# Fused four-layer graph network on one core: the tile pairs of the last layer in two interleaved streams, each with its own accumulation bank

## The reference

```
deg = jnp.maximum(adj.sum(axis=1, keepdims=True), 1e-08)
w = adj / deg
log_ij = _logmap(x[:, None, :], x[None, :, :], c)
agg = jnp.einsum('ij,ijc->ic', w, log_ij)
transformed = agg @ weight + bias
origin = jnp.zeros_like(transformed)
return _expmap(origin, transformed, c)
```

## Time and profile before

| | us |
|---|---|
| median of 3 runs (1842.58 to 1855.55) | 1851.97 |
| the profiled execution | 1837.7 |
| its span in the profile | 1835.9 |
| PE busy / DVE busy / ACT busy / POOL busy | 1602.7 / 1369.7 / 908.6 / 296.4 |
| first sum (L1849) of the last layer's loop, start | 1303.23 |
| last sum, start | 1774.94 |
| first of the final transposes (L1021), start | 1787.83 |

### The profile page before, as it was taken

The page is one execution under the profiler, slowest core; times in us unless marked ns, Lnnn a source line. Parts: engine busy times, 40 slices in busy tenths (PEclk is TensorE's granted clock), DMA queues, the critical chain, the costliest instruction groups (busy, mean ns, idle before and its releaser), DMA issues.

```text
span 1835.9 us, 21795 instructions
## 1 busy us (share of the span) xinstructions
PE 1602.7 (87%) x8154; PEld 660.7 (36%) x8198; DVE 1369.7 (75%) x1602; ACT 908.6 (49%) x870; POOL 296.4 (16%) x190
## 2 busy tenths in 40 slices
PE   6999999999997899999999863876789999999990
PEld 2433333333334344434334332332432333333340
DVE  4777799978885666785885945997447778878877
ACT  2233567733333323333332314221547789988964
POOL 1000000000000122111120200000423334444440
PEclk9999999999997899999999996998556779989995
DMA  9999599849994255243343110336012435454610
GB/s 351 412 413 413 206 374 392 335 151 414 413 393 186 95 181 183 93 140 135 137 146 119 55 46 13 137 126 206 12 47 80 138 127 195 149 182 139 202 40 23
DMA packets 118012, 348.72 MB, mean 190 GB/s; under 512 B 6244, under 2 KB 31144, under 8 KB 117672
## 3 DMA queue, kind: packets, MB, share of 16 engines
q1 hardware_dynamic: 106784, 329.27, 48.7%
q10 hardware_dynamic: 11144, 18.34, 2.7%
HBM read 329.76 MB, written 17.83 MB: 189 GB/s over the span
## 4 chain that ended last, share of the span: by engine, by line
PE 44%; DVE 26%; issue 16%; POOL 9%; ACT 2%; DMA 1%; SPq 0%; DVEq 0%; POOLq 0%; ACTq 0%
PE ps L751 10%; POOL ring L648 9%; PE ps L821 9%; PE ps L828 6%; DVE work L1476 5%; DVE work L1725 4%; DVE work L1513 4%; PE ps L684 3%; PE ps L683 3%; PE ps L924 2%; PE ps L796 2%; DMA ring<-in_adjT 1%; DVE ring L1681 1%; DVE work L1678 1%; PE ps L800 1%
## 5 line engine op out<-in xcount | busy, mean ns | idle before, releaser
L821 PE MATMUL ps<-ring,stage_f 128*64 128x512 f32 x512 | 264.2, 598 | 33.8 <-DVE ring L1681 29.3
L823 PE MATMUL ps<-work,stage_f 128*64 128x512 f32 x512 | 264.2, 598 | 0.0
L1084 ACT ACTIVATE work<-ps,code_bias 128x1024 uint8<-128x1024 f32 x128 | 135.7, 1110 | 243.6 <-PE ps L684 237.0
L1170 ACT ACTIVATE work<-ring 128x2048 f32<-128x2048 f32 x64 | 122.3, 1913 | 236.9 <-PE ps L830 230.5
L648 POOL TENSOR_TENSOR ring<-ring,work 128x1024 f32<-128x1024 f32 x80 | 189.4, 2367 | 286.2 <-DVE work L1842 232.9
L828 PE MATMUL ps<-work,stage_words 128*64 128x512 bf16 x768 | 208.3, 380 | 0.0
L830 PE MATMUL ps<-work,stage_words 128*64 128x512 bf16 x768 | 208.3, 380 | 0.0
L924 PE MATMUL ps<-work 69*128 69x512 f32 x320 | 192.6, 732 | 1.9 <-DVE work L1768 1.9
L621 POOL COPY stage_f<-X 128x256 f32 (+1 forms) x32 | 30.9, 964 | 952.4 <-ACT work L1046 583.8
L751 PE MATMUL ps<-ring,work 128*64 128x512 f32 x704 | 160.8, 598 | 0.0
L828 PEld LDWEIGHTS ps<-work,stage_words 128*64 128x64 bf16 x768 | 84.8, 110 | 178.1 <-issue 153.4
(11 more groups left out here) (289 smaller groups left out, 2910.5 us busy)
## 6 DMA issues: line engine op xcount, KB each, us to landing
ring<-in_adjT SPq DMA_DIRECT2D x90, 2048.0 KB, 10.8
work<-in_adjT SPq DMA_DIRECT2D x26, 2048.0 KB, 13.0
ring<-in_adjT SPq DMA_DIRECT2D x48, 1024.0 KB, 7.1
codes<-work ACTq DMA_DIRECT2D x64, 256.0 KB, 6.2
work<-codes SPq DMA_DIRECT2D x32, 512.0 KB, 3.6
ring<-in_adjT SPq DMA_DIRECT2D x32, 512.0 KB, 3.8
X<-in_x ACTq DMA_DIRECT2D x1, 1024.0 KB, 5.0
work<-in_xT SPq DMA_DIRECT2D x2, 512.0 KB, 22.4
```

Of the source, the lines that this page charges most:

```text
L821: nc.tensor.matmul(ps[0:F, h, :], stage_f[:, t, k, 0:F], ring[:, r, k, cols], start=start, stop=stop)
L823: nc.tensor.matmul(ps[F:P, h, :], stage_f[:, t, k, 0:F], negs[:, pair, i, cols], start=start, stop=stop)
L1084: nc.scalar.activation(codes[:, u, k:k + 2, :].rearrange("p k c -> p (k c)"), ps[:, bank:bank + 2, :].rearrange("p k c -> p (k c)"), ACT.Relu,
L1170: nc.scalar.activation(negs[:, pair], ring[:, s % RING, 2 * pair:2 * pair + 2, :], ACT.Relu, scale=-1.0).then_inc(negs_made, 1)
```

## The change

The units are now two streams, 48 off (O) and 32 own (D), each sorted by I, and taken in the pattern O O D O D from the first to the last five, which are O O O D D. So units of different I are mixed. Each stream accumulates its gathers in a bank of its own: off in bank 4, own in bank 5. Since the result of a quarter is now complete in two parts, they are added into `aggT`, which is cleared first (a memset of 128x2048 on VectorE), in seven additions instead of four copies. Bank 5 was one of the two banks for transposed halves, so both halves now go through bank 6, and `move_x` goes through bank 7 only and stands at the end of the TensorE period.

```diff
-        folded = [(fold_lo, fold_hi), (fold_odd[:, 0:4, :], fold_odd[:, 4:8, :])]
+        folded = [(fold_odd[:, 0:4, :], fold_odd[:, 4:8, :]), (fold_lo, fold_hi)]
...
-        for I in range(NQ):
-            for turn in range(CB):
-                for J, k in [divmod(turn * I + i, CB) for i in range(I)] + [(I, turn)]:
-                    u = Unit(len(units), J, I, k)
...
+        off_left = [(J, I, k) for I in range(NQ) for J in range(I) for k in range(CB)]
+        own_left = [(I, I, k) for I in range(NQ) for k in range(CB)]
+        units, off_units, own_units = [], [], []
+        for five in range(UNITS // 5):
+            for kind in "OODOD" if five < UNITS // 5 - 1 else "OOODD":
+                left, stream = (off_left, off_units) if kind == "O" else (own_left, own_units)
+                u = Unit(len(units), *left.pop(0))
...
+            u.sums = 4 if u.off else 5
...
-        POINTS_AT = [CB - 1] + [u.n + 2 for u in own_units[CB:CB + 2]]
+        POINTS_AT = [1, 8, 11]
...
             def distances(u):
-                if u.first:
+                if u.n == 0:
                     pe.wait_ge(ut_copied, u.I + 1)
...
             def move_x(n):
-                if n >= 2:
-                    pe.wait_ge(moved_kept, n - 1)
+                if n:
+                    pe.wait_ge(moved_kept, n)
...
-                    mm = nc.tensor.matmul(ps[:, 5 + n % 2, c * F:(c + 1) * F], UT[0:F, b * P:(b + 1) * P], w3_sb[:],
+                    mm = nc.tensor.matmul(ps[:, 7, c * F:(c + 1) * F], UT[0:F, b * P:(b + 1) * P], w3_sb[:],
...
             def turn_g(u, h):
-                if u.offs:
-                    pe.wait_ge(mirror_weighted, 2 * u.offs - 1 + h)
-                else:
-                    pe.wait_ge(moved_kept, NQ)
+                if u.offs or h:
+                    pe.wait_ge(mirror_weighted, 2 * u.offs + h)
...
-                    mm = nc.tensor.transpose(ps[:, 5 + h, c * P:(c + 1) * P],
+                    mm = nc.tensor.transpose(ps[:, 6, c * P:(c + 1) * P],
...
             def gather(u):
-                if u.first:
-                    pe.wait_ge(points_made, 2 * (u.I + 1))
-                if u.first and u.I:
-                    pe.wait_ge(direct_added, u.I)
+                pe.wait_ge(points_made, 2 * (u.J + 1))
+                if u.first and u.kept_before:
+                    pe.wait_ge(direct_added, u.kept_before)
...
-                    mm = nc.tensor.matmul(ps[h * F:(h + 1) * F, 4, :], points[:, u.rows, :],
+                    mm = nc.tensor.matmul(ps[h * F:(h + 1) * F, u.sums, :], points[:, u.rows, :],
...
                 if unit_at(n + 1):
                     distances(units[n + 1])
-                if 1 <= n < 1 + NQ:
-                    move_x(n - 1)
                 if unit_at(n - 2):
                     gather(units[n - 2])
...
                 if off_at(n - 1):
                     turn_g(units[n - 1], 0)
+                if 1 <= n < 1 + NQ:
+                    move_x(n - 1)
...
-            def keep_direct(u):
+            def add_direct(u):
                 dve.wait_ge(gathered, u.n + 1)
-                V.tensor_copy(aggT[:, u.I * HALF:(u.I + 1) * HALF], ps[:, 4, :]).then_inc(direct_added, 1)
+                wait_for_sums()
+                sums = aggT[:, u.I * HALF:(u.I + 1) * HALF]
+                V.tensor_tensor(sums, sums, ps[:, u.sums, :], ALU.add).then_inc(direct_added, 1)
...
+            V.memset(aggT[:], 0.0).then_inc(sums_cleared, 1)
             make_points(0)
...
-                if 3 <= n < 3 + NQ:
-                    keep_moved(n - 3)
+                if 2 <= n < 2 + NQ:
+                    keep_moved(n - 2)
```

More of the change, by code:

```diff
@@ L207, in __init__ @@
                 self.banks = 2 * (n % 2)
-        units = []
-        off_units, own_units = [], []
-        for I in range(NQ):
-            for turn in range(CB):
-                for J, k in [divmod(turn * I + i, CB) for i in range(I)] + [(I, turn)]:
-                    u = Unit(len(units), J, I, k)
[L215 to L218, removed]
+        off_left = [(J, I, k) for I in range(NQ) for J in range(I) for k in range(CB)]
[5 more added lines that the diff above has]
+                u = Unit(len(units), *left.pop(0))
+                u.place = len(stream)
+                stream.append(u)
+                units.append(u)
+        for stream in (off_units, own_units):
+            for u, before, after in zip(stream, [None] + stream, stream[1:] + [None]):
+                u.first = not before or before.I != u.I
+                u.last = not after or after.I != u.I
+        ends = [u for u in units if u.last]
+        for stream in (off_units, own_units):
+            done = 0
+            for u in stream:
+                u.kept_before = done
+                if u.last:
+                    done = ends.index(u) + 1
         for u in units:
-            u.first = u.n == 0 or units[u.n - 1].I != u.I
-            u.last = u.n == UNITS - 1 or units[u.n + 1].I != u.I
+            u.sums = 4 if u.off else 5
             u.edges = ring[:, 0, u.place % 4, :] if u.off else ring[:, 1, u.place % 2, :]
@@ L980, in mirror_products @@
                         pe.wait_ge(mirror_added, quad)
+                    else:
+                        pe.wait_ge(moved_kept, NQ)
                 for c in (2 * i, 2 * i + 1):
@@ L1012, in _ @@
                     turn_g(units[n - 1], 0)
+                if 1 <= n < 1 + NQ:
+                    move_x(n - 1)
             pe.wait_ge(sum_made, UNITS)
-            pe.wait_ge(direct_added, NQ)
+            pe.wait_ge(direct_added, len(ends))
             pe.wait_ge(mirror_added, len(quad_ends))
@@ L1782, in mirror_weights, with wait_for_sums @@
                         dve.wait_ge(mirrored, u.quad - 1)
-                V.tensor_tensor(folded[u.quad % 2][h][:, :, u.cols], ps[:, 5 + h, :].rearrange("p (b c) -> p b c", c=P),
+                V.tensor_tensor(folded[u.quad % 2][h][:, :, u.cols], ps[:, 6, :].rearrange("p (b c) -> p b c", c=P),
                                 strip(u.quad)[:, h * GB:(h + 1) * GB, u.cols], ALU.mult).then_inc(mirror_weighted, 1)
-            def keep_direct(u):
+            sums_added = [0, 0]
+            def wait_for_sums():
+                dve.wait_ge(sums_cleared, 1)
+                for added, times in zip((direct_added, mirror_added), sums_added):
+                    if times:
+                        dve.wait_ge(added, times)
+            def add_direct(u):
                 dve.wait_ge(gathered, u.n + 1)
-                V.tensor_copy(aggT[:, u.I * HALF:(u.I + 1) * HALF], ps[:, 4, :]).then_inc(direct_added, 1)
+                wait_for_sums()
+                sums = aggT[:, u.I * HALF:(u.I + 1) * HALF]
+                V.tensor_tensor(sums, sums, ps[:, u.sums, :], ALU.add).then_inc(direct_added, 1)
+                sums_added[0] += 1
             def add_mirror(quad, u):
                 dve.wait_ge(mirrored, quad + 1)
-                dve.wait_ge(direct_added, u.J + 1)
-                if quad:
-                    dve.wait_ge(mirror_added, quad)
+                wait_for_sums()
                 first = u.J * HALF + quad % 2 * 2 * P
-                V.tensor_tensor(aggT[:, first:first + 2 * P], aggT[:, first:first + 2 * P], ps[:, 7, 0:2 * P],
-                                ALU.add).then_inc(mirror_added, 1)
+                sums = aggT[:, first:first + 2 * P]
+                V.tensor_tensor(sums, sums, ps[:, 7, 0:2 * P], ALU.add).then_inc(mirror_added, 1)
+                sums_added[1] += 1
             def keep_moved(n):
@@ L1834, in _ @@
                 if v and v.last:
[L1835 removed]
+                    add_direct(v)
                 if n - 7 in quad_ends[:-1]:
@@ L1864, in _ @@
             add_mirror(len(quad_ends) - 1, units[quad_ends[-1]])
-            dve.wait_ge(direct_added, NQ)
+            dve.wait_ge(direct_added, len(ends))
             dve.wait_ge(mirror_added, len(quad_ends))
```

5 lines of the change are left out of this document (3 added, 2 removed).

## The result

The changed kernel takes 1859.05 us (median of 17 runs, 1853.18 to 1868.43), the kernel before 1851.97 (17 runs, 1836.71 to 1860.79). The ratio is 1.0055, with a 95% interval of 1.003 to 1.0081: slower by half a per cent, beyond the noise of the comparison but within the 1% that the prediction called no change. The executions of before fall in two groups, five from 1836.71 to 1842.58 and twelve from 1850.42 to 1860.79, and the ratio goes by their mean, so it stands for +10 us where the medians differ by 7; for the same reason ratios and medians differ in the experiments too. The profiled execution took 1857.29 us with a span of 1855.6.

The account below looks back on a forecast made before the run. Some 5.1 us a unit was taken as the full-clock floor, with low clock and the start above it. Terms +2 + 0 + 23 - 2.6 = +22 to 23 us on 1847 made 1870 us; range 1846 to 1892.

Parts of the forecast that it names:

- within 1%: Whole kernel: the time differs from before by no more than about 1% (18.5 us); chance 0.42.
- slower by more than 1%: Whole kernel: over about 18.5 us slower, with six falls of the clock and more; chance 0.51.
- three signs of a wrong forecast: Loop: clock over 0.93, no slow period among the five, or first eight units under 68 or over 84 us.
- The bottom of the range: Whole kernel: four falls of the clock less the spread of the start, 1847 + 5 - 4, about 1846 us.
- The start ahead of the loop: Before the first sum: unit 0's first distances also need the second node copy, +2.0 us.
- so it is hidden, just: Ahead of the node copies: clearing `aggT`, 1.80 us, fits where VectorE idles 1.79 us.
- The first eight units: Start of the loop: the gather leaves the move chain but O units add transposes; 0, from -6 to +6 us.
- The pace at full clock: Loop after the start: four units at 5.01 and one at 6.1 us for the single bank, 5.23 a unit.
- The clock: Loop: six falls to low clock in product-free stretches at 7 us each, 42 us.
- The end: After the loop: last products fill the last gather's wait for GpSimd, -2.6 us.
- The base: Whole kernel: the sum is set on 1847 us, the mean of four known executions.
- every product-free stretch goes cold: Loop, a rival: eleven falls of the clock, +58 us, 1905 us; nine falls and more had chance 0.17.

Follow-up runs that it names:

- e1_old_order: The changed kernel with its units back in the old order (eight D, then O D, O O D, O O O D): 1869.13 us, ratio to before 1.0145.
- e2_one_bank: The kernel before with both transposed halves through bank 6, its order of units kept: 1882.90 us, ratio 1.0199.
- e3_fill: The changed kernel with one set of four transposes done twice in each period without mirror products: 1833.51 us, ratio to before 0.9954.
- e5_before_fill: The kernel before with one set of four transposes done twice in every period without mirror products: 1825.61 us, ratio 0.9854.
- e6_before_fill_start: The kernel before with transposes doubled in product-free periods, plus eight unread identity transposes in start periods without transposes or moves: 1818.50 us, ratio 0.981.
- e4_spread: The changed kernel with a quad's mirror products spread over six periods instead of four, no work added: 1857.44 us, ratio to before 1.0031.

## Why the prediction was right or wrong

- *The size, 1870 for 1859, and the side.* The sum was +22 to 23, the profiled parts give +16.7 (and +13.5 in the second profile: loop +14.3, start +2.9, end -3.7), the medians +7 and the ratio +10. The time lay in the range and in the case "within 1%", which had 0.42; "slower by more than 1%" had 0.51, so the likelier side was missed. None of the three signs of a wrong forecast showed: the loop's clock was 0.82, the slow period is there, and the first eight units took 73.02 us.
- *One period too many.* From the first sum to the last there are 79 periods, eight and 71; the 471.7 us are counted so, but the forecast took 72 behind the first eight. Counted right, its terms give 76 + 71 x 5.23 + 42 = 489.3 us for the loop, where the profile has 489.1, and +17 in all. The 5 us that the sum was over are this slip. The bottom of the range was added up loosely as well: by the forecast's own figures four falls are +9, and 1847 + 9 - 4 is 1852, not 1846.
- *The start ahead of the loop, +2.0:* +3.0. The second node copy cost 1.3 where 2.0 was said. The step that failed is "so it is hidden, just": the memset took 1.76 us as sized and used up VectorE's idle time, but a copy of 8 columns behind it now fell under GpSimd's operation and took 1.00 us, where it had taken 0.17. So the first node copy began 11.84 us after the small memset and not 10.80. Clearing cost 1.7; the rest of that goes with the first distances, which had 2.59 us before and took 3.61 in e1_old_order and 3.75 here (3.78 is their time at half clock).
- *The first eight units, 0 from -6 to +6:* -2.7. One period is 13.6 and one 11.9 us, and the early O units did raise the clock, for moments, from 1358 us on.
- *The pace at full clock, 5.23 with a 6.1 us period in five:* the period is there and the wait is the one named. From sum to sum it is 6.13 us where products fall into it and 6.3 where none do, which the sum left out; a group of five at full clock is then 26.35 us (6.29, 4.90, 5.13, 5.04, 4.99), 5.27 a unit.
- *The clock, 42 us:* the 71 periods took 416.12 us, at 5.23 they would be 371.3, so 44.8 (at the 5.27 of the full-clock groups it would be 42). The total is right, its makeup only in part: after the eighth unit there were twelve stretches at half clock in place of six. Read in steps of 1 us they last 6, 4, 13, 11, 3, 14, 3, 4, 24, 3, 4 and 24 us. Against the periods of a group at full clock, the two of 24 us cost some 9 us each and the three of 11 to 14 some 5 each, the seven short ones together some 9. So five of them count, near the number said, but the price was not 7; that number times price fits is luck.
- *The end, -2.6:* -3.7. The wait for GpSimd is gone, and the products ran at full clock (1.00 from 1801.50 to 1805.20), where it was 0.78 over the last products of before.
- *The attribution.* Here the reasoning, though not the sum, went wrong. The single bank was priced at 0.1 to 0.2 us a unit, and the low clock was laid on the even mix. The mix costs nothing once the rest of the change is there, and may gain some 4 to 10 us (1869 to 1859 in the medians). The 71 periods have nearly the same clock in either order, 0.88 and 0.87. The bank by itself costs 32 us in the old order; what it costs in the new one was not tried. The comparison that misled me was between the pace of before, 5.11 to 5.21, and 5.23, as if the order alone lay between them. With the single bank, in the old order, the full-clock periods of e2_one_bank make 5.4 a unit in O O D (6.14, 5.04, 4.99, 6.28, 4.90, 5.13) and more in O O O D. So the bank costs in the old order, and the new order, with one pair of O units in five, gives part of it back.
- *The base.* I set the sum on the mean of four executions, 1847. Two profiles of before, 1837.7 and 1838.3, were both executions of the faster group, while 14 us more is usual. The sum on the median, 1852, would have been 1875 and further off. That the difference of the medians, 7, is smaller than that of the loops, 14 to 17, is not settled: the two kernels' executions seem to differ in how long the layers ahead take, and two profiles of each can't tell.
- *The rivals.* That every product-free stretch goes cold came true in part: the clock fell in all six stretches of three periods and in two of the five of two, eight of eleven (in three of them twice; the twelfth low stretch lies ahead of the first products). The price was not the 7 us each of that rival. That transposes do not bring the full clock, as the Trainium skill's page "TensorE: Matmul & The Clock Gate", Part 4, has it, is refuted by three kernels here: transposes added without use raised the clock of the loop from 0.87 to 0.96 (e3_fill), kept it up all the way (e5_before_fill), and raised it at the start (e6_before_fill_start).

## What to carry to other kernels

A bank taken from a double buffer costs where two of its users meet, and what costs is less the wait itself than what is queued behind it on the same engine: look at the next instruction in that queue (here the push, and behind it the whole chain of a period). It costs a second time where the clock falls more often with it. Before reordering for balance, ask in which periods the clock falls and what TensorE lacks in them; useless transposes put there were worth 26 us here, more than any reordering that was tried. And sum a forecast on more than one profile: here the unchanged layers moved by more than the change.

## What was not expected of the hardware

- TensorE idle or lightly loaded is not the only road to low clock: it was busy 14.60 of 14.60 us at 0.50, and 23.02 of 23.90 in the fall shown above. Busy time read at half clock says little, since the same work takes up to twice as long there (`distances` 3.78 us against 1.98); but the clock also fell out of a stretch in which TensorE was busy 6.97 of 7.90 us at 0.97. What lifted the clock in e3_fill, e5_before_fill and e6_before_fill_start was transposes added; e4_spread lifted it from 0.87 to 0.92 with no work added.
- Two small operations of VectorE and GpSimd were both slower where they overlapped: the copy of 8 columns took 1.00 us and GpSimd's L647, begun at 1292.69, took 3.73, where the same operation took 2.76 when it next ran, at 1297.60. Before, they did not overlap and took 0.17 and 2.77. The Trainium skill's page "SBUF — State Buffer", section "Who interferes with whom", describes a port pair that the two share and that one of them holds for a whole instruction, the other waiting. That both took longer agrees with a shared pair. That GpSimd, which issued first, held it for its whole instruction does not come out of the rows: the copy ended at 1294.71, and L647 at 1296.42. The memset and the node copies overlapped L647 too, and no run here took them apart.
- Kernels with the same layers ahead of the loop had its first sum anywhere from 1303 to 1325 us, of which the change itself answers for 3.
